# A decoder of two layers on one core: semaphore clears on five engines, earlier X^T copies on ACT, and a new order of the first steps of three phases

## What is computed

```
x = norm(x + gqa attention(x))              # 16 heads of 32, 4 key heads, rotary by head index
x = norm(x + latent attention(x, ctx))      # 16 heads, weights folded to 64 columns a head
x = norm(x + ternary ffn(x))                # w1, w2, w3 quantised to -1, 0, 1; hidden 1408
x = norm(x + decay attention(x))            # linear attention, no softmax
x = norm(x + causal cross attention(x, ctx))# softmax, keys and values from ctx
x = norm(x + moe(x) + shared ffn(x))        # top 2 of 8 experts, hidden 352; shared hidden 704
```

## Time and profile before

| what | value |
|---|---|
| timed runs | 2261.15, 2266.09, 2271.64 us |
| the profiled execution's own time | 2257.88 us |
| its span, first to last instruction | 2256.1 us |
| mean granted TensorE clock | 0.946 of full |
| busy: PE, weight load, DVE, ACT, POOL | 1998.7, 1620.9, 1076.1, 712.7, 346.1 us |

### The profile page before, as it was taken

How to read it: one execution, slowest core, us unless ns; L and a number is a source line. 1 busy time by engine, 2 the same in 40 slices (tenths; PEclk the granted TensorE clock), 3 DMA queues, 4 the chain that set the end, 5 groups by cost and what they waited for, 6 DMA issues and landing times. The chain is left out here.

```text
span 2256.1 us, 32905 instructions
## 1 busy us (share of the span) xinstructions
PE 1998.7 (89%) x12204; PEld 1620.9 (72%) x12204; DVE 1076.1 (48%) x1877; ACT 712.7 (32%) x2272; POOL 346.1 (15%) x308
## 2 busy tenths in 40 slices
PE   5899958899999988999799997898967999899990
PEld 4767736778888857777677875676756777799990
DVE  5566743345454546433454445566765232222226
ACT  1555622334344432222131101344542121233322
POOL 1111100000000018200021100000002400544315
PEclk9999968999999999999899998899988999999995
DMA  5001124000000013000092002000013200444236
GB/s 183 18 22 39 40 105 146 32 1 1 1 1 1 1 43 112 1 0 0 27 335 86 1 1 66 1 1 1 1 42 117 112 0 0 170 164 155 82 102 196
DMA packets 61436, 135.88 MB, mean 60 GB/s; under 512 B 6256, under 2 KB 24048, under 8 KB 59376
## 3 DMA queue, kind: packets, MB, share of 16 engines
q1 hardware_dynamic: 36240, 94.14, 11.9%
q0 software_dynamic: 5840, 27.92, 3.5%
q10 hardware_dynamic: 19216, 11.89, 1.9%
HBM read 90.68 MB, written 43.25 MB: 59 GB/s over the span
## 5 line engine op out<-in xcount | busy, mean ns | idle before, releaser
L1210 PE MATMUL banks<-ternary_xth,ternary_wq 128*128 (+1 forms) x352 | 138.5, 394 | 1.4 <-DVE ternary_xtl L73 1.4
L1210 PE MATMUL banks<-ternary_xtl,ternary_wq 128*128 (+1 forms) x352 | 138.3, 393 | 0.0
L409 ACT ACTIVATE gqa_pr<-banks,gqa_nb 128x128 f32<-128x128 f32 x256 | 90.1, 379 | 60.8 <-DVE gqa_nb L545 60.8
L409 ACT ACTIVATE causal_pr<-banks,causal_nb 128x128 f32<-128x128 f32 x256 | 90.1, 378 | 56.8 <-DVE causal_nb L545 56.8
L100 PE MATMUL banks<-latent_vh,latent_cth 128*128 128x512 f32 x256 | 104.2, 407 | 3.5 <-DVE latent_ctl L923 3.5
L100 PE MATMUL banks<-weights,expert_xgh 128*128 x312 | 104.6, 335 | 2.7 <-DVE expert_xgl L1732 2.4
L101 PE MATMUL banks<-weights,expert_xgh 128*128 x312 | 101.2, 325 | 0.0
L102 PE MATMUL banks<-weights,expert_xgl 128*128 x312 | 101.1, 324 | 0.0
L102 PE MATMUL banks<-latent_vh,latent_ctl 128*128 128x512 f32 x256 | 100.1, 391 | 0.0
L101 PE MATMUL banks<-latent_vl,latent_cth 128*128 128x512 f32 x256 | 100.1, 391 | 0.0
L880 ACT ACTIVATE latent_pt<-banks 128x1024 f32<-128x1024 f32 x32 | 32.9, 1027 | 194.4 <-PE banks L1021 194.4
(11 more groups left out here) (427 smaller groups left out, 5616.1 us busy)
## 6 DMA issues: line engine op xcount, KB each, us to landing
x_slots<-decay_zeros SPq DMA_DIRECT2D x39, 256.0 KB, 3.0
y_slots<-decay_zeros SPq DMA_DIRECT2D x39, 256.0 KB, 3.3
expert_xin<-x_slots SPq DMA_DIRECT2D x39, 256.0 KB, 2.9
y_slots<-expert_ys SPq DMA_DIRECT2D x39, 256.0 KB
weights_raw<-in_expert_experts SPq DMA_DIRECT2D x4, 2176.0 KB, 8.8
gqa_tw<-in_ternary_w ACTq DMA_DIRECT2D x4, 2112.0 KB, 10.9
ternary_raw<-in_ternary_w SPq DMA_DIRECT2D x11, 768.0 KB, 4.2
expert_raw<-in_expert_experts POOLq DMA_DIRECT2D x3, 2176.0 KB, 9.5
```

Source lines behind the costliest of these rows:

```text
L409: a = act.activation(pr[:, h, c, :], S.bank[2 * h + c // 4][:, (c % 4) * P:(c % 4 + 1) * P], ACT.Exp, bias=nb[:, h, c:c + 1], accum_out=su ...
L1210: a = pe.matmul(dst[:, :], wq[:, j, m, c * P:(c + 1) * P], x[:, c, toks], start=c == 0 and n == 0, stop=c == C - 1 and n == 1)
```

## The change

Four things change. (1) The clears of a phase are dealt out over SyncE, ACT, DVE, GpSimd and PE, every fifth to each. (2) ACT walks its own order `act_plan`, in which an `x` or `c` step that directly follows `S` or `lo` is moved ahead of them. (3) In latent the high half of `kr` is made right ahead of the first `k` step, as is the low half; DVE rotates two blocks of ctx at the first `c` and the rest in four pieces at the `fv` of folds 4 to 7; the rotation's scratch is `pt`. (4) In ternary only four blocks are transposed ahead of the body; the other twelve are transposed inside the first group's steps (two in each of steps 0 and 1, one in each of steps 2 to 9), through banks that those steps leave free. In shared the 16 transposes use eight banks; the low half of the first weights is made in four quarters among the router's groups; the rank matmuls move behind `up` of step 1; and the first half's loop is written out.

```diff
-    def on_pe(self, pe):
+    def on_pe(self, pe, t):
         S = self.S
-        for t in range(B):
-            if t >= 2:
-                pe.wait_ge(self.lo, t - 1)
-            for c in range(C):
-                m = pe.transpose(S.bank[t % 2][:, c * P:(c + 1) * P], S.X[:, t, c * P:(c + 1) * P], S.ident[:, :])
-            m.then_inc(self.full, 1)
+        for c in range(C):
+            m = pe.transpose(S.bank[self.bank_of(t)][:, c * P:(c + 1) * P], S.X[:, t, c * P:(c + 1) * P], S.ident[:, :])
+        m.then_inc(self.full, 1)
...
                 @block.sync
                 def _(sp):
-                    for s in self.sems:
+                    for s in self.sems[0::5]:
                         sp.sem_clear(s)
+
+                @block.scalar
+                def _(act):
+                    for s in self.sems[1::5]:
+                        act.sem_clear(s)
...
+        act_plan = list(plan)
+        for k, e in enumerate(act_plan):
+            j = k
+            while e[0] in ("x", "c") and act_plan[j - 1][0] in ("S", "lo"):
+                act_plan[j], act_plan[j - 1] = act_plan[j - 1], act_plan[j]
+                j -= 1
...
-            for e in plan:
+            for e in act_plan:
...
-        t1, t2 = (t[:, 0, :, :].rearrange("p t (b n) -> p (t b) n", n=P) for t in (qt, kt))
+        t1, t2 = pt[:, 0:4, :], pt[:, 4:8, :]
+        turned = {("c", 0, 0): (0, 2)} | {("fv", 4 + k, 0): (2 + 4 * k, min(6 + 4 * k, B)) for k in range(4)}
...
-            act.wait_ge(kr_in, 16)
-            act.activation(krh[:, :], kr, ACT.Copy).then_inc(kr_hi, 1)
             for e in plan:
                 what, b, i = e
+                if e == ("k", 0, 0):
+                    act.wait_ge(kr_in, 16)
+                    act.activation(krh[:, :], kr, ACT.Copy).then_inc(kr_hi, 1)
...
-            dve.wait_ge(kv_in, 32)
-            rotate(0, GB)
-            dve.wait_ge(kv_rot, 1)
-            dve.wait_ge(kr_hi, 1)
-            dve.tensor_tensor(krl[:, :], kr, f32(krh[:, :]), ALU.subtract).then_inc(kr_lo, 1)
             for e in plan:
                 what, b, i = e
-                if e == ("fm", 0, 0):
-                    rotate(GB, B)
+                if e in turned:
+                    if e == ("c", 0, 0):
+                        dve.wait_ge(kv_in, 32)
+                    else:
+                        dve.wait_ge(kv_rot, list(turned).index(e))
+                    rotate(*turned[e])
+                if e == ("k", 0, 0):
+                    dve.wait_ge(kr_hi, 1)
+                    dve.tensor_tensor(krl[:, :], kr, f32(krh[:, :]), ALU.subtract).then_inc(kr_lo, 1)
... (ternary)
+        xt = Transposer(S, xth, xtl, sem, lambda t: t if t < 2 * GT else 2 + t % 2)
+        beside = [[4, 5], [6, 7]] + [[t] for t in range(2 * GT, B)] + [[]] * (J - 10)
...
                         act.activation(sg[:, j % 2, :], gate[j % 2][:, :], ACT.Sigmoid).then_inc(sig_done, 1)
+                        if first:
+                            for t in beside[j]:
+                                xt.on_act(act, t)
...
-            for t in range(B):
+            for t in range(GT):
                 xt.on_dve(dve, t)
-                if t in (B // 2, B - 1):
-                    compare(0 if t < B - 1 else 1)
+            compare(0)
...
                 for j in range(J + 1):
+                    if first and j < J:
+                        for t in beside[j]:
+                            xt.on_dve(dve, t)
+                        if j == 0:
+                            compare(1)
...
                     ups(gate[j % 2], 0, j).then_inc(gate_full, 1)
                     if j >= 2:
                         pe.wait_ge(hf_done, g * J + (j - 1))
+                    if first:
+                        for t in beside[j]:
+                            xt.on_pe(pe, t)
+                        if j == 2:
+                            pe.wait_ge(xt.lo, 2 * GT)
                     if j >= 2:
                         down(j - 2)
+                    if first and j >= 2 and beside[j]:
+                        pe.wait_ge(xt.lo, beside[j][-1] + 1)
                     ups(up[j % 2], 1, j).then_inc(up_full, 1)
... (shared)
+        xt = Transposer(S, xth, xtl, sem, lambda t: t % 8)
+        CUT = [k * WE // G for k in range(G + 1)]
...
                 dve.tensor_copy(sg[0:E, g % 2, :], gate[g % 2][0:E, :]).then_inc(rt_copied, 1)
+                dve.wait_ge(w_hi, 1)
+                a = dve.tensor_tensor(wel[:, 0, CUT[g]:CUT[g + 1]], raw[:, CUT[g]:CUT[g + 1]],
+                                      f32(weh[:, 0, CUT[g]:CUT[g + 1]]), ALU.subtract)
+            a.then_inc(w_lo, 1)
...
-            dve.wait_ge(w_hi, 1)
-            dve.tensor_tensor(wel[:, 0, :], raw[:, :], f32(weh[:, 0, :]), ALU.subtract).then_inc(w_lo, 1)
...
+            for t in range(B):
+                if t >= 8:
+                    pe.wait_ge(xt.lo, t - 7)
+                xt.on_pe(pe, t)
...
-            pe.wait_ge(given_done, 1)
-            pe.matmul(yb[0][:, 0:B * E], before[:, :], ...
+            def ranks():
+                pe.wait_ge(given_done, 1)
+                pe.matmul(yb[0][:, 0:B * E], before[:, :], ...
...
                         ups(up[q % 2], s, F1 + j * P, FT[j], toks).then_inc(up_full, 1)
-                        if q >= 1:
+                        if s == 0 and m == 0:
+                            if q == 1:
+                                ranks()
+                            if q == 2:
+                                pe.wait_ge(slots_done, 1)
+                                down(0)
+                        if q >= 1 and not (s == 0 and m == 0 and q == 1):
                             down(q - 1)
```

More of the change, by code:

```diff
@@ L72, in on_dve @@
         cols = slice(t * P, (t + 1) * P)
-        dve.tensor_tensor(self.xtl[:, :, cols], four(self.S.bank[t % 2]), f32(self.xth[:, :, cols]),
+        dve.tensor_tensor(self.xtl[:, :, cols], four(self.S.bank[self.bank_of(t)]), f32(self.xth[:, :, cols]),
                           ALU.subtract).then_inc(self.lo, 1)
@@ L1237, in body @@
                 down(J - 1)
+                if first:
+                    pe.wait_ge(xt.lo, B)
             over_tokens(pe, body)
@@ L1299, in down_w, with halves @@
             return t[0:FT[j], s, WU + j * DM:WU + (j + 1) * DM]
+        def halves(eng, s):
+            if s == 0:
+                yield from range(G // 2)
+            else:
+                with eng.Fori(0, G // 2) as m:
+                    yield m
         def over_experts(eng, body):
@@ L1343, in body @@
                 act.activation(weh[:, 1 - s, :], raw[:, :], ACT.Copy).then_inc(w_hi, 1)
-                with act.Fori(0, G // 2) as m:
+                for m in halves(act, s):
                     t = m * Q
@@ L1453, in body @@
                 dve.tensor_tensor(wel[:, 1 - s, :], raw[:, :], f32(weh[:, 1 - s, :]), ALU.subtract).then_inc(w_lo, 1)
-                with dve.Fori(0, G // 2) as m:
+                for m in halves(dve, s):
                     t = m * Q
@@ L1526, in body @@
             def body(s, last):
-                with pe.Fori(0, G // 2) as m:
+                for m in halves(pe, s):
                     pe.wait_ge(w_lo, s + 1)
```

44 lines of the change are left out of this document (26 added, 18 removed).

## The result

| | before | after |
|---|---|---|
| median of the timed runs, this comparison | 2264.57 us (4 runs) | 2209.76 us (4 runs, 2205.99 to 2212.43) |
| ratio, 95% interval | | 0.9759 (0.9743 to 0.9775) |
| a second comparison, changed kernel again | 2264.28 us (17 runs) | 2207.71 us (5 runs), 0.9761 (0.9744 to 0.9779) |
| the profiled execution: time, span | 2257.88, 2256.1 us | 2212.43, 2210.6 us |
| mean granted clock of that execution | 0.946 | 0.953 |

The change saves 54.6 us (0.0241 x 2264.57; 51 to 58 by the interval); the forecast was 2209 us. The two profiled executions lie only 45.5 us apart: that of before is faster than its four timed runs, that of after is the slowest of its four.

What follows compares the result with a forecast made beforehand. PE, busy in 89% of the span, was taken as the bound, with its idle and lower-clock time to win. Clears 11, order 27, latent 2, ternary 5, shared 12 sum to 57 us: 2201 profiled, 2209 us median, range 2188 to 2230.

Steps and rivals of the forecast that it cites:

- the other low half: gqa block 4: DVE makes one other low half of about 0.6 us before X^T's, done at 121.3.
- the clock term: Six x steps of gqa and causal: projections back at the upper clock, 1.9 us a place, 11 us.
- Rival A: x steps: stalls go but the clock doesn't come back, short pauses remain; 11 us less won, 2220 us; chance 0.14.
- D: x steps: the exponentials' order does not matter, x itself being transposed too late; 2236 us; chance 0.04.
- the `kr` wait: Latent, behind fold 2: fold's copy, ACT's kr copy and DVE's subtraction make a new wait of 2.9 us before k.
- the second q: Latent: rotation pieces ahead of the low halves of folds 4 to 7 make PE some 1.7 us late there.
- B: Overlapped starts give nothing in ternary and latent, shared wins half; 2222 us, ternary group over 88 us; chance 0.13.
- F: Ternary's first group waits each step at 1.2 GHz throughout; 2284 us, group of 140 us or more; chance 0.02.
- one more slow start: Ternary: two slow starts of the clock, 1.6 us each, one more than before; costs 1.6 us.
- E: Ternary: port lock, every compare meets a GpSimd instruction and takes 1.18 us; 10 us more, 2219 us; chance 0.05.
- an idle 8 us: Shared: PE idle before `up` of step 2, which then runs at the lower clock, 2 us lost.

Runs made afterwards that it cites:

- e6: Changed kernel with the clears dealt by their price per engine, PE getting 5 of 43 and SyncE 11; 2202.79 us, ratio 0.9719.
- e2: Kernel before with only ACT's order changed, copies of X^T ahead of the exponentials; 2234.72 us, ratio 0.9869.
- e10: Kernel before, meant to keep PE busy with 14 products in the six stalls; the condition was never true, none added; 2261.71 us, ratio 0.9996.
- e7: Changed kernel with latent's kr halves moved ahead of fold 2 and rotation pieces to DVE's idle places; 2203.98 us, ratio 0.9713.
- e11: Changed kernel with ACT's copy of fm in latent moved ahead of the exponentials before it; 2207.33 us, ratio 0.9758.
- e8: Changed kernel with shared's hf of steps 0 and 1 made first on DVE and the second weights' subtraction quartered; 2200.66 us, ratio 0.9712.

## Why the prediction was right, and where its terms were off

The total held (57 predicted, 54.6 measured), and so did the mechanisms of clears, order, latent and shared; ternary gained what was predicted for another reason than its sum says. That the total came so close is in part luck: the clears were 3.9 us too high and the order and shared 2.7 and 1.8 too low. The sizes part by part:

| part | predicted | measured |
|---|---|---|
| clears | 10.9 (8 to 13.8) | 7.0 (4.1 to 10.0), 7.7 by the gaps |
| ACT's order | 27 (14 to 31) | 29.7 (24.7 to 34.6) |
| latent | 2 (-4 to 7) | 1.5 at the first scores, 2.7 in the phase's mean length, not resolved |
| ternary | 5 (-3 to 9) | 5.4 (2.7 to 8.2) |
| shared | 12 (5 to 15) | 13.8 (8.8 to 19.0) |

**Clears.** The step that failed is the price on the other engines. I took SyncE's 55 ns for all. In the changed kernel SyncE drains after nine clears at gqa's end, PE 0.6 us later after eight. The step from 8 clears to 5 (e6) prices one on PE at 0.12 us, an estimate from the drains, and in e6 the drains come together. The lower bound I had, twice SyncE's price (8 us saved), was the nearer one, and the times are still 1 us below it.

**ACT's order.** The arithmetic of the place held but for one term. 3.0 us were predicted per stall at blocks 4 and 8. In causal it is 3.0 (3.65 less 0.63). In gqa the projection starts 2.4 us sooner behind the transposes (3.2 us, not 5.6): I took the other low half as 0.6 us, "one of the pair of 1.29", but it is a single instruction of 1.30 us there. So the waits are 1.25 us, not under 1 as forecast, and the six stalls gave some 18 us, not 19. The 12 products run in 2.9 us, not 5.3. What I took for the clock term, 11 us, was low: 8.0 us in causal and about 8 in gqa (16.1 lost in the mean of five profiles with the old order, 8.1 in that of nine with the new). Rival A, in which short pauses keep the clock down, is refuted: in all nine profiles with the new order the 4 us behind the waits of 1.25 and 0.63 us at blocks 4 and 8 are at 1.00 (36 places). D is refuted by e2. But gqa has two levels of lost clock with the same code, 5.4 to 5.9 and 9.9 to 12.0 us: that is 6 us of chance in a run, and no part of the change decides it.

The Trainium skill, "TensorE: Matmul & The Clock Gate", section "HAM oscillation", describes half rate behind a gap of PE. The traces agree: in the profile of before the 4 us behind each of the six waits of 3.65 us are at 0.50 to 0.58, and at blocks 4 and 8, where the wait is 1.25 or 0.63 us now, they are at 1.00. That the gap is the cause is argued from this pairing; e10, which was to part the two, didn't.

**Latent.** k was to come 6 us earlier and came 5.7 earlier; ctx was to suffer from the folds asked for sooner, and landed 1.4 us later in three profiles of five; the `kr` wait was to be 2.9 and is 2.77; the second q was to be 1.7 us late and waits 2.65 in place of 1.02. The 2 us that the sum left are 1.5 at the first scores. The Trainium skill, "DMA: Bandwidth & Descriptors", section "Queues, rings and completion order", has the engines turn between queues by packets; I had made up to 4 us of it. The traces agree in direction, with 1.4 us, where DVE waited for ctx at all. That the term is right doesn't make the edit worth much: the clock behind the next wait of 2.73 us varies by more than it (e7).

**Ternary.** The first product was to come 7 us after the start and came after 8.6 (GpSimd's first `below` starts 5.6 us after the start, at 832.3, not 4.2); the first group was to be 83 us long, counted to its last down product (87.7 before), and is 83.5 counted to the residual sum (910.21 - 826.67), which was 86.8 before: 3.3 us less in this pair, 4.7 in the mean of all profiles. B (88) and F (140) are refuted. The step that had it wrong is the clock's: the sum took 1.6 us for one more slow start, a size that no row shows, and in the runs most of the moved transposes and the waits beside them stand at the upper clock and 6 us less are lost to the lower one. PE's idle time in the group didn't fall: the waits moved from between the transposes into the steps, and the gain is the clock's. The compare's median is 747 ns and its maximum 1180, as before, so E is as well.

**Shared.** The first router product is 13.0 us after the start, where the working has 20 less 7 (the prediction's last part says "20 us to the router's end becomes 13 less", which doesn't fit its own working; the 20 us are those to the first product); the router ends 26.9 us after it, forecast 26; ranks take 3.7 us, as forecast. The `up` of step 2 was to start 52.5 us after the start, behind an idle 8 us at the lower clock; it started after 56.4, behind 8.02 us, at the lower clock (0.43 us a product). The 4 us come from steps 0 and 1, which start 2 us late and have eight products at the lower clock. They didn't cost the total, and that is luck: the old kernel's shared phase was longer in every other profile (259.9 to 262.9) than in the one that the sum was made against (257.2).

## What to carry to other kernels

An in-order engine that has both a short copy that others wait for and a long batch that nobody waits for soon should do the copy first; look for it as a repeated PE wait behind "low half of a copy" with the batch ahead of the copy in the timeline. Then look at what stands second in the same queue: in e11 the wait went from the first operation of the chain to the next one and nothing was won, in e8 the whole chain was moved and some 10 us came. Before believing a phase's few us from one pair of profiles, split each phase into PE's idle time and the time lost to the lower clock over several profiles: here the first was steady to 1 to 5 us for the same code, the second varied by up to 13.

## What the runs showed of the hardware that was not expected

- A semaphore clear costs some 0.12 us on PE against 0.055 on SyncE (estimates from the drains above); dealt by price the engines end within 0.1 to 0.2 us of each other at six of seven phase ends.
- A DVE subtraction of two SBUF tiles, 128x512, took 1.30 us beside an addition on GpSimd and 0.68 without it; at two places of gqa that is 0.6 us of PE's wait.
- With the same code, the clock lost in one phase has separate levels from run to run: 5.4 to 5.9 or 9.9 to 12.0 us in gqa with the new order. Behind the same 2.73 us wait in latent, with the old code in seven profiles, 1.7 to 10.2 us were lost.
- Parts of a few us add up within their intervals although they share the clock: 7.0 + 29.7 + 5.4 + 13.8 = 55.9 (about 8 either way) against 54.6 for all with the latent part.
